# A fused attention and feed-forward block: fewer masking columns in the scores, another PSUM bank for the transposed inputs, and a new order on four engines

## The reference

```
x = x + tanh(g_x) * attention(layernorm(x), ctx)     # 16 heads of 16, causal
x = x + tanh(g_f) * ffn(layernorm(x))                # silu(gate) * up, 256 -> 1024 -> 256
```

## Time and profile before

| What | Value |
|---|---|
| Time, median of 3 runs | 1727.05 us (1724.25 to 1727.05) |
| Profiled execution, its own time | 1726.53 us |
| Span of its instructions | 1724.8 us |
| PE busy | 1604.0 us (93%) |
| PEld busy | 1305.7 us (76%) |
| DVE busy | 1442.1 us (84%) |
| ACT busy | 1352.3 us (78%) |
| POOL busy | 1142.5 us (66%) |
| Granted TensorE clock, mean | 0.989 |

### The profile page before, as it was taken

How to read it: one execution, slowest core, us unless ns; L and a number is a source line. 1 busy time by engine, 2 the same in 40 slices (tenths; PEclk the granted TensorE clock), 3 DMA queues, 4 the chain that set the end, 5 groups by cost and what they waited for, 6 DMA issues and landing times. The chain is left out here.

```text
span 1724.8 us, 45975 instructions
## 1 busy us (share of the span) xinstructions
PE 1604.0 (93%) x15430; PEld 1305.7 (76%) x15430; DVE 1442.1 (84%) x3097; ACT 1352.3 (78%) x3145; POOL 1142.5 (66%) x1873
## 2 busy tenths in 40 slices
PE   3699999999999999999999999999999999999985
PEld 2577777777778778777777877877777787787763
DVE  5288888888888888888888888888888888888884
ACT  2388888888788888888878888888888888888873
POOL 3567667676776766767677677676666767766632
PEclk9899999999999999999999999999999999999997
DMA  3322232223223223222322322322332232232210
GB/s 119 108 96 84 93 102 97 87 95 111 82 85 111 84 90 106 89 95 94 108 88 84 111 84 87 108 85 95 99 102 89 88 111 84 84 111 84 86 41 13
DMA packets 116600, 158.31 MB, mean 92 GB/s; under 512 B 14608, under 2 KB 66960, under 8 KB 116368
## 3 DMA queue, kind: packets, MB, share of 16 engines
q1 hardware_dynamic: 115088, 155.24, 27.3%
q10 hardware_dynamic: 1280, 0.14, 0.1%
HBM read 37.88 MB, written 16.78 MB: 32 GB/s over the span
## 5 line engine op out<-in xcount | busy, mean ns | idle before, releaser
L818 DVE TENSOR_REDUCE row_max<-psum 128x8 f32<-128x1024 f32 x256 | 311.6, 1217 | 19.4 <-PE psum L477 19.0
L690 ACT ACTIVATE s_low<-psum,row_max 128x128 f32<-128x128 f32 x1024 | 279.1, 400 | 0.3 <-DVE row_max L818 0.3
L697 ACT ACTIVATE prob_t<-psum 128x1024 f32<-128x1024 f32 x256 | 271.6, 1061 | 2.1
L487 PE MATMUL psum<-ident,s_low 128*128 128x128 f32 x2048 | 265.3, 272 | 0.7 <-ACT s_low L682 0.7
L995 POOL TENSOR_TENSOR ln<-ln,minus_half 128x1 f32<-128x1 f32 x128 | 70.2, 549 | 256.4 <-DVE ln L867 256.4
L487 PEld LDWEIGHTS psum<-ident,s_low 128*128 128x128 f32 x2048 | 230.7, 141 | 2.4 <-issue 1.1
L477 PE MATMUL psum<-k_stk,q_stk 128*128 128x256 f32 x1024 | 210.9, 328 | 0.0
L705 ACT ACTIVATE th<-psum,sm 128x512 f32<-128x512 f32 x256 | 179.7, 702 | 18.7 <-PE psum L578 17.8
L578 PE MATMUL psum<-wg_t,xq_t 128*128 128x512 f16 x512 | 154.0, 382 | 42.1 <-ACT x_f L715 22.8
L477 PEld LDWEIGHTS psum<-k_stk,q_stk 128*128 128x128 f32 x1024 | 158.4, 190 | 37.0 <-DMA k_stk<-k_t 0.3
L846 DVE TENSOR_TENSOR h<-gu,psum 128x512 f32<-128x512 f32 x256 | 175.8, 687 | 8.9
(11 more groups left out here) (112 smaller groups left out, 3682.8 us busy)
## 6 DMA issues: line engine op xcount, KB each, us to landing
k_stk<-k_t SPq DMA_DIRECT2D x384, 128.0 KB, 2.3
q_stk<-q_t SPq DMA_DIRECT2D x192, 256.0 KB, 2.5
c_in<-in_ctx SPq DMA_DIRECT2D x64, 256.0 KB
x_in<-in_x SPq DMA_DIRECT2D x64, 256.0 KB
out<-y SPq DMA_DIRECT2D x128, 128.0 KB
g_nat<-in_L_ffn_w_gate SPq DMA_DIRECT2D x1, 1024.0 KB, 8.6
g_nat<-in_L_ffn_w_up SPq DMA_DIRECT2D x1, 1024.0 KB, 11.0
g_nat<-in_L_ffn_w_down SPq DMA_DIRECT2D x1, 1024.0 KB, 12.9
```

Source lines behind the costliest of these rows:

```text
L487: last = nc.tensor.transpose(S_B[half][:, n * P:(n + 1) * P], s_low[:, HPC * half + n, :], ident[:, :])
L690: last = nc.scalar.activation(s_low[:, HPC + n, :], S_B[1][:, n * P:(n + 1) * P], ACT.Identity, bias=row_max[:, HPC + n:HPC + n + 1])
L697: nc.scalar.activation(prob_t[:, HPC * half:HPC * (half + 1), :].rearrange("p h k -> p (h k)"), S_B[half], ACT.Exp).then_inc(p_ok[half], 1)
L818: nc.vector.tensor_reduce(out=row_max[:, HPC * half:HPC * (half + 1)], in_=S_B[half].rearrange("p (h k) -> p h k", k=P), axis=AX.X, op=ALU ...
```

## The change

It has three parts, and constants that go with them.

**The mask.** The mask matmuls write only keys 32 to 127 of each head: 4 x 96 columns in place of 512. Keys 0 to 31 are masked by the spare row: in `k_stk` spare row k holds 1.0 at key k, and in `q_stk` it holds -2^100 at the queries q < k, so that the q.k matmul adds the mask itself. The spare rows are set once, at the start, by four `affine_select` on POOL (two over 4096 elements a partition, two over 2048). The mask's constant is -2^100 in place of -1e30.

**The bank.** IN_T is bank 5 in place of 4. `inputs_t` now waits for `gu_ok[1]` of the section before, in place of `xqt_ok`, and the wait for ACT's copy of it stands before the UP matmuls in place of the GATE matmuls.

**The order.** The lists of calls of PE, ACT, DVE and POOL are written in another order. That of SP is as before.

```diff
-        IN_T, B6, B7 = bank(4), bank(6), bank(7)
+        IN_T, B6, B7 = bank(5), bank(6), bank(7)
...
+                    k_rows = k_stk[n][:, :, :, :, :, :].rearrange("p a h c s k -> p (a h c s) k")
+                    q_rows = q_stk[n][:, :, :, :, :].rearrange("p h c s q -> p (h c s) q")
+                    nc.gpsimd.affine_select(out=k_rows, in_=k_rows.bitcast(F32), compare_op=ALU.not_equal, fill=1.0, base=FREE,
+                                            pattern=[[0, 4 * HB * DC], [STEP, P]], channel_multiplier=-1).then_inc(vz, 1)
+                    nc.gpsimd.affine_select(out=q_rows, in_=q_rows.bitcast(F32), compare_op=ALU.is_ge, fill=MASKED, base=FREE,
+                                            pattern=[[0, 2 * HB * DC], [STEP, P]], channel_multiplier=-1).then_inc(vz, 1)
...
                     for b in range(2):
-                        nc.tensor.matmul(S_B[half][:, b * BANK:(b + 1) * BANK], ident_b[:, :],
-                                         causal[:, :].unsqueeze(1).to_broadcast((P, 4, P)),
+                        late = S_B[half][:, b * BANK:(b + 1) * BANK].rearrange("p (h k) -> p h k", k=P)[:, :, PAIR_HD:P]
+                        nc.tensor.matmul(late, ident_b[:, :],
+                                         causal[:, PAIR_HD:P].unsqueeze(1).to_broadcast((P, 4, P - PAIR_HD)),
                                          start=True, stop=False, skip_group_check=True)
...
-                    if c.ffn:
-                        pe.wait_ge(xqt_ok, c.tile(2))
+                    wait(pe, gu_ok[1], c.tile(3))
...
-                        if c.projects:
-                            pe.wait_ge(ctx_cp if c.s == 0 else xn_cp, c.pair(0))
...
                     for dst, w in ((GATE, wg_t), (UP, wu_t)):
+                        if half == 0 and dst is UP and c.projects:
+                            pe.wait_ge(ctx_cp if c.s == 0 else xn_cp, c.pair(0))
```

More of the change, by code:

```diff
@@ L606, in body @@
                     if c.s == 0:
+                        if c.projects:
+                            inputs_t(c)
                         if c.ffn:
@@ L610, in body @@
                             scores(c.t, 1)
+                        if c.ffn:
+                            gate_up(c, 0)
                         if c.outp:
                             out_natural(c)
-                        if c.projects:
-                            inputs_t(c)
                         if c.down:
@@ L754, in body @@
                             quant_t(c)
+                        if c.projects:
+                            inputs_t(c)
                         if c.attn:
                             shift_first(c)
-                        if c.projects:
-                            inputs_t(c)
+                        if c.ffn:
+                            tanh(c, 0)
                         if c.down:
@@ L762, in body @@
                             out_t(c)
-                        if c.ffn:
-                            tanh(c, 0)
                         if c.attn:
                             shift(c)
+                        if c.ffn:
+                            tanh(c, 1)
+                        if c.attn:
                             exp(c, 0)
@@ L790, in body @@
                         if c.attn:
-                            shift(c)
+                            exp(c, 0)
                         if c.ffn:
@@ L922, in body @@
                             shift(c)
+                            top(c, 1)
                         if c.outp:
                             out_natural(c)
[L925 to L953, removed]
                         if c.ffn:
@@ L965, in body @@
                             row_scales(c)
+                        if c.ffn:
+                            hidden_scales(c)
+                    else:
+                        if c.attn:
+                            top(c, 0)
+                            shift(c)
+                        if c.norm:
+                            first_norm(c)
+                        if c.outp:
+                            out_natural(c)
+                        if c.ffn:
+                            gated(c, 0)
+                        if c.outp:
+                            out_t(c)
+                        if c.down:
+                            result(c)
+                        if c.attn:
+                            top(c, 1)
+                        if c.outp:
+                            residual(c)
+                        if c.ffn:
+                            gated(c, 1)
+                        if c.outp:
+                            row_scales(c)
+                        if c.ffn:
+                            hidden_scales(c)
                         if c.norm:
                             norm_stats(c)
-                        if c.ffn:
-                            hidden_scales(c)
                 walk(dve, body)
```

59 lines of the change are left out of this document (29 added, 30 removed).

## The result

The changed kernel takes 1681.51 us (median of 4 runs, 1679.55 to 1682.67) against 1727.05. The ratio is 0.974 (95% interval 0.972 to 0.976). The profiled execution took 1679.55 us, its span 1677.8, 47.0 less than before. The forecast was 1675, with 1654 to 1702 as the range.

A forecast was written before the change was run, and what follows sets the result against it. PE's in-order queue was taken as the bound: its columns plus five short waits. Old stalls 1.69 + mask 0.43 - new stalls 1.05 and 0.18 = 0.89 us a pair over 61 pairs, less 4 us margin: 1675 us, range 1654 to 1702.

The forecast's parts named there:

- five short waits: Stalls in PE's in-order queue in each pair of one even and one odd section, together 1.69 us of 25.40.
- Waits a, c and d: PE waiting for ACT's copies: gate matmuls 0.22 us (even) and 0.54 (odd), `inputs_t` 0.17 (odd); all to go.
- b: Even section, PE before gate-and-up half 1, waiting for DVE's h: 0.44 us, to go with the new order.
- `down` becomes the wait: PE before `down`, on ACT's h_t: start 4.45 us into both sections, new stalls 1.05 us (even) and 0.18 (odd).
- the sum: Saving per pair: 1.69 old stalls + 0.43 mask - 1.05 - 0.18 new stalls = 0.89 us, a pair of 24.51.
- The mask, 0.43 us a pair: Eight mask matmuls a pair on PE each lose 128 of 512 columns, 0.054 us each; 27.5 us over all 512.
- The thin margin on ACT, worth 4 us: Row maxima reach ACT's `shift_first` at most 0.03 to 0.1 us late; 4 us given back over 122 sections.
- Rival 3: Slower than before: late first row maxima delay `down` in full in both sections; up to 1749 us; chance 0.06.
- rival 2: The order only trades stalls, 0.4 us a pair added, 1699 us; or DVE's queue limits; 0.20 shared with another rival.
- Rival 1: The mask pays little: 96-column runs have a price or columns aren't the pace; 1693 to 1702 us; chance 0.12.
- Rival 4: Better than the walk: earlier h_t or shorter `hidden_t` tail, 0.1 to 0.2 us a section, 1657 us; chance 0.09.
- The spare rows are hidden: Setup: POOL's four affine_selects take 19 us within its 25.51 us of idle time; cost 0, range 0 to 3.

The follow-up runs named there:

- Run 3: The changed kernel with the full 512-column mask back and no spare rows; 1699.25 us, ratio 0.984, a pair 24.98 us.
- run 4: The kernel before with the mask's part and the bank, in the old order; 1681.18 us, ratio 0.974, a pair 24.63 us.
- run 2: The kernel before with the bank alone, full mask and old order; 1698.51 us, ratio 0.984, a pair 24.94 us.
- Run 5: The changed kernel with one extra DVE copy ahead of the first row maxima in each section; 1685.58 us, ratio 0.976, a pair 24.72 us.
- run 9: POOL's `centre` put ahead of `first_norm` in the even section: on run 7's kernel 1664.91 us, pair 24.38; on the changed kernel 1678.65 us, pair 24.63.
- run 7: The changed kernel with the even section's shifted-score transposes moved between `hidden_t` and `out_t`; 1670.9 us, ratio 0.969, a pair 24.53 us.
- run 1: The kernel before with the mask's and spare rows' edit alone; 1712.55 us, ratio 0.992, a pair 25.14 us.

## Why the prediction was right, and where it was off

- **PE's queue bounds the kernel, by columns and five short waits.** Right. The bank alone and the mask alone each moved the time.
- **Waits a, c and d go, and b with the order; `down` becomes the wait.** Right, in place and size: 4.45 and 4.44 us into the sections, 1.06 and 0.18 of stall against 1.05 and 0.18. That it fits to 0.01 is in part luck. `hidden_t` takes 0.45, not 0.53: in the earlier trace rows the next row had waited for DVE's o_n. `inputs_t` behind the values takes 0.50, not 0.44, and gate and up 0.88, not 0.86. The errors cancel, and `hidden_t` ends at 3.17 for 3.18. Run 3, without the mask, has 25.41 - 24.98 = 0.43 us a pair from bank and order; the sum had 1.69 - 1.23 = 0.46.
- **The mask, 0.43 us a pair.** The term that was mis-sized: 0.34 in the new order, 0.27 in the old one. The four score blocks lost their 0.11 each, as forecast. The values behind two of them step 0.05 longer, and in the old order waits that don't hang on the scores took more (with the new bank in the old order the mask gives 0.30, run 4 against run 2). This 0.09 of the 0.12 us by which the pair's saving fell short (0.77 for 0.89) is the larger part of the 6.5 us.
- **The thin margin on ACT, worth 4 us.** Wrong in size, and the row maxima it hung on were late: they start 0.38 us into the odd section, not by 0.17. I read `shift_first` as 1.20 us, from its start to the start of the next row. But the next row, the copy c_f, waited there for PE's transposes, which end at 907.05 and are seen 0.18 later. The step was 1.01, and that paid for the late maxima. Run 5 found 0.14 us of margin where I had 0.03. Rival 3's size was not reached, but its mechanism is real: where run 5's maxima came 0.35 later still, `down` came 0.36 later.
- **That order and bank belong together.** The prediction priced them as one term. Run 4 shows what this hid: the order alone is worth nothing, it trades stalls, as rival 2 said for the whole sum. Bank and mask carry all 45 us. Rival 2's other mechanism, that DVE's queue sets the pair, doesn't hold in the changed kernel (run 9: 24.63 against 24.64) and does in part once PE's stall is filled.
- **Rival 1, a mask that pays little:** no price of the four runs of 96 columns shows in the score blocks, which step by their columns; whether the longer step of the values behind them is one stays open. **Rival 4:** the stall can't be filled by PE alone, but by 0.12 us (run 7) and 0.26 us (run 9) a pair together with DVE's chain.
- **The spare rows are hidden.** Right for POOL's queue, 11.7 us in place of 19. Wrong as a mechanism: I looked at POOL's idle time alone, and DVE stood behind POOL's affine_selects, which cost 2 to 3 us of setup in eight of ten profiles. That the loop of the changed kernel's profile starts as early as before is luck of its start times; the range had these 3 us in it, for another reason.

## What to carry to other kernels

A stall that is taken away is worth what the next wait on the same queue leaves of it: here 0.93 us of measured waits gave 0.47, and 0.43 us of work gave 0.27 alone. Before you take a duration from the start of one row to the start of the next, look whether the second row waited for something. And when a filled stall gives little, look for the loop that closes over the other engines; its length between two like events (here result to result, on DVE) tells what can still be won. An engine with idle time of its own may still hold up another: look at the other engines' durations, not only at its queue.

## What the hardware showed that I had not expected

- POOL's two-operation instruction on 128x256 float32 took 1218 ns with subtract and multiply, 548 ns with add and multiply [the kernel before, L989, the same shapes]. Which property of the instruction costs it, the operation or the scalar's tile, wasn't tried.
- An affine_select on POOL over 4096 elements took 3.84 us, little more than a memset of the same size (3.51), while one of 128 elements took 0.29 against 0.20.
- PE's 32 small matmuls of the values step 1.06 us directly behind the short mask's score block, 1.01 behind the full one's, and 1.02 in run 1 where the projection of v stands between.
- DVE's copy of 128x256 float32 within SBUF took 0.28 us in the setup of the kernel before, and 2.9 to 3.9 us in eight profiles in which it started during POOL's affine_select of 4096 elements; in each it ended 0.14 to 0.15 us after that instruction. DVE's reduction of 2048 elements that overlapped POOL's affine_selects kept its 2.3 us.
- With one DVE instruction more in each section (run 5), DVE stood still for some 0.35 us at the same place every eight pairs, with no releaser in the profile. In the changed kernel such stalls are rare. What they are wasn't tried.
